# Window attention and MLP, second block: attention output kept by token, 32-row column tiles, input split moved to GpSimd

## What is computed

```
xn  = layernorm(x) ; windows of 8 x 8 tokens (49 to an image, 1568 in all)
qkv = xn @ w_qkv + b_qkv ; 6 heads of 16 features ; q = q / sqrt(16)
p   = softmax(q k^T)                # over the window's 64 keys, per head
x1  = x + (p v) @ w_proj + b_proj
out = x1 + gelu(layernorm(x1) @ w_fc1 + b_fc1) @ w_fc2 + b_fc2     # 384 hidden
```

## Time and profile before

| | us |
|---|---|
| median of 3 runs of the kernel before | 7315.32 |
| lowest and highest of the 3 | 7312.77, 7322.0 |
| span of the profiled execution (its own time; what lies around the span is not recorded) | 7322.4 |
| busy in the span: PE, PE weight loads | 7021.7, 5453.8 |
| busy in the span: DVE, ACT, POOL | 6310.8, 6294.8, 5480.1 |
| first matmul of the second block's set-up | 4462.4 |

### The profile page before, as it was taken

The page is one execution under the profiler, slowest core; times in us unless marked ns, Lnnn a source line. Parts: engine busy times, 40 slices in busy tenths (PEclk is TensorE's granted clock), DMA queues, the critical chain, the costliest instruction groups (busy, mean ns, idle before and its releaser), DMA issues. The chain is left out here.

```text
span 7322.4 us, 312543 instructions
## 1 busy us (share of the span) xinstructions
PE 7021.7 (96%) x110894; PEld 5453.8 (74%) x110894; DVE 6310.8 (86%) x13114; ACT 6294.8 (86%) x11444; POOL 5480.1 (75%) x6349
## 2 busy tenths in 40 slices
PE   6999999999999999999999995999999999999998
PEld 4777777777777777777777774777777777777777
DVE  5888888888888888888888885888888888888886
ACT  5999999999998999999999995877887877877877
POOL 3777777777777777777777775777777777777776
PEclk9999999999999999999999997999999999999999
DMA  0111111111111111111111111111111111111111
GB/s 21 29 30 30 30 29 30 29 29 30 30 30 29 30 30 29 30 30 30 29 30 30 30 26 27 44 44 44 44 44 44 44 44 43 44 44 44 45 44 36
DMA packets 367610, 252.62 MB, mean 34 GB/s; under 512 B 271816, under 2 KB 347336, under 8 KB 366152
## 3 DMA queue, kind: packets, MB, share of 16 engines
q1 hardware_dynamic: 366154, 233.04, 12.4%
HBM read 78.64 MB, written 77.07 MB: 21 GB/s over the span
## 5 line engine op out<-in xcount | busy, mean ns | idle before, releaser
L879 POOL TENSOR_TENSOR swin_score<-swin_score,swin_top 113x588 f32<-113x588 f32 x1024 | 1203.1, 1175 | 744.2 <-DVE swin_top L751 743.5
L622 ACT ACTIVATE swin_probT<-swin_ps_probs 128x339 f32<-128x339 f32 x2048 | 922.0, 450 | 198.7 <-PE swin_ps_probs L479 177.4
L479 PE MATMUL swin_ps_probs<-swin_ident,swin_prob 113*128 113x113 f32 x6144 | 991.8, 270 | 6.7 <-ACT swin_probT L622 6.7
L1564 POOL TENSOR_TENSOR plain_prob<-plain_prob,plain_inv_total 128x384 f32<-128x384 f32 x784 | 634.4, 830 | 450.1 <-DVE plain_inv_total L1477 450.1
L479 PEld LDWEIGHTS swin_ps_probs<-swin_ident,swin_prob 113*128 113x128 f32 x6144 | 667.9, 141 | 355.1 <-issue 320.7
L746 DVE TENSOR_TENSOR swin_score<-swin_ps_scores,swin_bias_tab 113x588 f32<-113x588 f32 x1024 | 777.9, 760 | 175.1 <-PE swin_ps_scores L469 173.8
L751 DVE TENSOR_REDUCE swin_top<-swin_score 113x12 f32<-113x588 f32 x1024 | 769.0, 751 | 0.2
L628 ACT ACTIVATE swin_prob<-swin_score 113x588 f32<-113x588 f32 x1024 | 719.0, 702 | 5.8 <-POOL swin_score L879 2.9
L782 DVE SCALAR_TENSOR_TENSOR swin_x<-swin_y,swin_y_rstd,swin_x_res 98x96 f32<-98x96 f32 x1024 | 601.7, 645 | 0.8 <-POOL swin_y_rstd L897 0.7
L1289 PE MATMUL plain_ps_dense<-plain_w_fc,plain_hid 128*128 128x96 f32 x4704 | 589.1, 275 | 2.2 <-ACT plain_hid L1362 2.2
L493 PEld LDWEIGHTS swin_ps_mixed<-swin_probT,swin_v_heads 128*32 128x32 f32 x24576 | 422.3, 109 | 222.2 <-issue 145.7
(11 more groups left out here) (188 smaller groups left out, 20880.6 us busy)
## 6 DMA issues: line engine op xcount, KB each, us to landing
swin_k_heads<-swin_k_hat SPq DMA_DIRECT2D x1024, 36.8 KB
plain_x_in<-between_blocks SPq DMA_DIRECT2D x784, 48.0 KB, 2.2
plain_k_heads<-plain_k_hat SPq DMA_DIRECT2D x392, 96.0 KB, 2.1
out_dram<-plain_x SPq DMA_DIRECT2D x784, 48.0 KB
swin_x_in<-in_x SPq DMA_DIRECT2D x224, 136.5 KB
between_blocks<-swin_x SPq DMA_DIRECT2D x224, 136.5 KB
swin_x_in<-in_x SPq DMA_DIRECT2D x224, 19.5 KB
between_blocks<-swin_x SPq DMA_DIRECT2D x224, 19.5 KB
```

Of the source, the lines that this page charges most:

```text
L479: last = nc.tensor.transpose(psP[:, n * QT:(n + 1) * QT], prob[0:QT, p, 2 * hp:2 * hp + 2, :].rearrange('p h k -> p (h k)'), ident[0:QT, 0 ...
L622: nc.scalar.activation(to, psP[:, 0:3 * QT], ACT.Copy).then_inc(did['probT'], 1)
L879: nc.gpsimd.tensor_tensor(view, view, bcast(top[0:QT, p % 2, :], 2, WIN), ALU.subtract).then_inc(did['shifted'], 1)
L1564: nc.gpsimd.tensor_tensor(pair, pair, bcast(inv_total[0:QT, p // 2, p % 2 * heads:(p % 2 + 1) * heads], 2, WIN), ALU.mult).then_inc(did['p ...
```

## The change

In the second block, on every group:

- **Mix by token.** The stationary factor is now 32 queries of `probT`, the moving one the 34 columns (`V`) of `v_heads` for a pair of heads: 16 features of each and two columns of ones, which give the sum of the exponentials of each head. The result is token-major in four column tiles of 32 rows, 48 matmuls to a group. DVE takes the reciprocal of the sums from PSUM and multiplies (`scale_mixed`), PE turns the result with four transposes (`turn_mixed`), and DVE copies it to `mixedT` (`copy_mixed`). `total` on DVE, `scale_probs` on POOL and `copy_mixed` on ACT are gone, and `turn_probs` waits for the exponentials themselves.
- **32-row column tiles.** Values, projection and MLP output are issued as matmuls with 32 stationary columns, into rows 0, 32, 64 and 96, instead of 64 or 128 stationary columns. The moving side stays (48, 96 and 96 columns).
- **Input's parts on POOL.** `high_x` goes from ACT and `low_x` from DVE to POOL, where the high part is the input times a column of ones, both from `xT` in SBUF.
- **Orders.** `turn_x1` now stands behind `queries` on PE (ahead of values and mix), values ahead of mix, and `turn_x` behind the MLP output. ACT, DVE and POOL are reordered to suit.

The core of the diff (waits of `turn_x` and `turn_x1` included):

```diff
@@ buffers and set-up
-    HB = J // 2
-    SUMS = 2 * HALF * 2
+    V = 2 * D + 2
...
+one = sb('one', [DIM, 1])
...
-v_heads = sb('v_heads', [128, 2, WINDOWS, BANDS, HB, 32])
+v_heads = sb('v_heads', [128, 2, WINDOWS, HP, V])
...
-total_of = sb('total', [128, 2, 2 * heads])
-inv_total = sb('inv_total', [128, 2, 2 * heads])
+inv_total = sb('inv_total', [128, PAIRS * HP, 2])
+mixed = sb('mixed', [128, PAIRS, DIM])
...
-    part = v_heads[odd * HALF:odd * HALF + WIN, buffer, 0, 0, 0, odd * D:(odd + 1) * D]
-    return bass.AP(part.tensor, part.offset, [list(part.ap[0]), [HB * 32, WINDOWS * BANDS], [32 + 2 * D, HB], [1, D]])
+    part = v_heads[odd * HALF:odd * HALF + WIN, buffer, :, :, odd * D:(odd + 1) * D]
+    return part.rearrange('r w n d -> r (w n) d')
...
+    nc.gpsimd.memset(one[:], 1.0)
...
+            ones = v_heads[odd * HALF:(odd + 1) * HALF, buffer, :, :, 2 * D + odd]
+            nc.vector.memset(ones.rearrange('r w n -> r (w n)'), 1.0)
@@ tensor engine
-            pe.wait_ge(did['mixedT'], upto(g + d - 1))
-            for w in range(WINDOWS):
-                p, half = divmod(w, 2)
-                for band in range(BANDS):
-                    last = nc.tensor.matmul(psO[32 * band:32 * band + 32, w * WIN:(w + 1) * WIN], v_heads[:, parity(d), w, band, 0, :], probT[:, p, band, half * HALF:half * HALF + WIN], start=True, stop=True)
+            pe.wait_ge(did['mixed'], upto(g + d - 1))
+            for p in range(PAIRS):
+                for hp in range(HP):
+                    for rows in range(0, TT, 32):
+                        last = nc.tensor.matmul(psO[rows:rows + 32, (p * HP + hp) * V:(p * HP + hp + 1) * V], probT[:, p, hp, rows:rows + 32], v_heads[:, parity(d), 2 * p + rows // HALF, hp, :], start=True, stop=True)
             last.then_inc(did['mixed_made'], 1)
 
+    def turn_mixed(d):
+        if exists(g + d, groups):
+            pe.wait_ge(did['mixed'], upto(g + d))
+            pe.wait_ge(did['xT_whole'], upto(g + 1))
+            for p in range(PAIRS):
+                last = nc.tensor.transpose(psT[0:DIM, p * TT:(p + 1) * TT], mixed[:, p, :], ident[0:TT, 0:TT])
+            last.then_inc(did['mixed_turned'], 1)
+
     def turn_probs(d, p):
         if exists(g + d, groups):
-            pe.wait_ge(did['prob_scaled'], upto(g + d, p, PAIRS))
+            pe.wait_ge(did['prob'], upto(g + d, p, PAIRS))
...
-            pe.wait_ge(did['xT'], upto(g + d))
+            pe.wait_ge(did['xT_whole'], upto(g + d))
             for w in range(WINDOWS):
                 for odd in range(2):
                     cols = w_qkv[:, 2 * DIM:3 * DIM].rearrange('c (h o d) -> c h o d', o=2, d=D)[:, :, odd, :]
-                    out = psM[odd * HALF:odd * HALF + WIN, bank, w * HP * D:(w + 1) * HP * D]
-                    last = nc.tensor.matmul(out, xT[:, parity(d), w * WIN:(w + 1) * WIN], cols, start=True, stop=True)
+                    for part in range(2):
+                        rows = odd * HALF + 32 * part
+                        first = w * WIN + 32 * part
+                        last = nc.tensor.matmul(psM[rows:rows + 32, bank, w * HP * D:(w + 1) * HP * D], xT[:, parity(d), first:first + 32], cols, start=True, stop=True)
...
-                last = nc.tensor.matmul(psM[0:TT, bank, p * DIM:(p + 1) * DIM], mixedT[0:DIM, parity(d), p * TT:(p + 1) * TT], w_proj[0:DIM, :], start=True, stop=True)
+                for rows in range(0, TT, 32):
+                    last = nc.tensor.matmul(psM[rows:rows + 32, bank, p * DIM:(p + 1) * DIM], mixedT[0:DIM, parity(d), p * TT + rows:p * TT + rows + 32], w_proj[0:DIM, :], start=True, stop=True)
...
-    def output(d, h, bank):
+    def output(d, bank):
         if exists(g + d, groups):
             pe.wait_ge(did['hid'], upto(g + d, CHUNKS - 1, CHUNKS))
-            for p in (2 * h, 2 * h + 1):
+            for p in range(PAIRS):
                 for c in range(CHUNKS):
-                    last = nc.tensor.matmul(psM[0:TT, bank, p * DIM:(p + 1) * DIM], hid[:, c, p * TT:(p + 1) * TT], w_fc2[:, c, :], start=c == 0, stop=c == CHUNKS - 1)
-            if h == 1:
-                last.then_inc(did['fc2_made'], 1)
+                    for rows in range(0, TT, 32):
+                        last = nc.tensor.matmul(psM[rows:rows + 32, bank, p * DIM:(p + 1) * DIM], hid[:, c, p * TT + rows:p * TT + rows + 32], w_fc2[:, c, :], start=c == 0, stop=c == CHUNKS - 1)
+            last.then_inc(did['fc2_made'], 1)
...
-            pe.wait_ge(did['x1T_low'], upto(g - 4))
-            pe.wait_ge(did['xT'], upto(g + d - 1))
+            pe.wait_ge(did['x1T_low'], upto(g - 3))
...
-            pe.wait_ge(did['xT'], upto(g + 2))
-            pe.wait_ge(did['x1T_low'], upto(g + d - 1))
+            pe.wait_ge(did['mixedT'], upto(g - 2))
...
     scores(0)
     turn_probs(-1, 2)
+    turn_mixed(-2)
     free(('hid', -4, 1, CHUNKS), ('x2', -5), ('v_heads', 0), ('k_hat', 0))
     keys(1, A)
     turn_probs(-1, 3)
     free(('hid', -4, 2, CHUNKS), ('x1', -3), ('q_hat', 0))
     queries(1, B)
-    mix(-1)
+    turn_x1(-3)
     free(('k_hat', 1), ('hid', -4, 1, CHUNKS), ('x2', -5), ('v_heads', 0))
     values(1, A)
-    turn_x(2)
+    mix(-1)
     free(('q_hat', 1), ('hid', -4, 2, CHUNKS), ('x1', -3))
     project(-2, B)
     free(('v_heads', 1), ('k_hat', 1), ('hid', -4, 1, CHUNKS), ('x2', -5))
-    output(-4, 0, A)
-    turn_x1(-3)
-    output(-4, 1, A)
+    output(-4, A)
+    turn_x(2)
     free(('x1', -2), ('q_hat', 1), ('hid', -4, 2, CHUNKS))
     hidden(-3, 0, B)
@@ scalar engine
-    def copy_mixed(d):
...
-            nc.scalar.activation(xT[0:DIM, parity(d), 0:NT], psT[0:DIM, 0:NT], ACT.Copy)
-    def high_x(d):
-        if exists(g + d, groups):
-            act.wait_ge(did['q_made'], upto(g + d - 2))
-            nc.scalar.activation(xT_high[:, parity(d), :], psT[0:DIM, 0:NT], ACT.Copy).then_inc(did['xT'], 1)
+            nc.scalar.activation(xT[0:DIM, parity(d), 0:NT], psT[0:DIM, 0:NT], ACT.Copy).then_inc(did['xT_whole'], 1)
...
     copy_turned(-1, 2)
     exponentials(0, 0)
     copy_turned(-1, 3)
     exponentials(0, 1)
-    copy_mixed(-1)
+    high_x1(-3)
     spread_values(1, A)
-    copy_x(2)
-    high_x(2)
     exponentials(0, 2)
     exponentials(0, 3)
-    high_x1(-3)
     act.preload_act_table_set(GELU_SET)
+    copy_x(2)
     gelu(-3, 0, B)
     copy_turned(0, 0)
@@ vector engine
-    def total(d, h):
...
+    def scale_mixed(d):
+        if exists(g + d, groups):
+            dve.wait_ge(did['mixed_made'], upto(g + d))
+            dve.wait_ge(did['mixed_turned'], upto(g + d - 1))
+            made = psO[:, 0:PAIRS * HP * V].rearrange('p (n c) -> p n c', c=V)
+            nc.vector.reciprocal(inv_total[:, :, :], made[:, :, 2 * D:V]).then_inc(did['inv_total'], 1)
+            dve.wait_ge(did['inv_total'], upto(g + d))
+            out = mixed[:, :, :].rearrange('p w (n o d) -> p (w n) o d', o=2, d=D)
+            nc.vector.tensor_tensor(out, made[:, :, 0:2 * D].rearrange('p n (o d) -> p n o d', d=D), bcast(inv_total[:, :, :], 3, D), ALU.mult).then_inc(did['mixed'], 1)
...
-    def low_x(d):
-        if exists(g + d, groups):
-            dve.wait_ge(did['xT'], upto(g + d))
-            dve.wait_ge(did['q_made'], upto(g + d - 2))
-            nc.vector.tensor_tensor(xT_low[:, parity(d), :], xT[0:DIM, parity(d), 0:NT], xT_high[:, parity(d), :].bitcast(F32), ALU.subtract).then_inc(did['xT_low'], 1)
+    def copy_mixed(d):
+        if exists(g + d, groups):
+            dve.wait_ge(did['mixed_turned'], upto(g + d))
+            dve.wait_ge(did['proj_made'], upto(g + d - 2))
+            nc.vector.tensor_copy(mixedT[0:DIM, parity(d), :], psT[0:DIM, 0:NT]).then_inc(did['mixedT'], 1)
...
     shift(0, 0)
+    copy_mixed(-2)
     shift(0, 1)
     bias_k(1, A)
     bias_q(1, B)
     shift(0, 2)
     shift(0, 3)
+    low_x1(-3)
     residual(-2, B)
-    total(0, 0)
-    low_x1(-3)
     partial_x1(-2)
     result(-4, A)
-    total(0, 1)
     moments_x1(-2)
     partial_x(3)
-    low_x(2)
+    scale_mixed(-1)
     moments_x(3)
@@ GpSimd
-    def scale_probs(d, p):
...
+    def high_x(d):
+        if exists(g + d, groups):
+            pool.wait_ge(did['xT_whole'], upto(g + d))
+            pool.wait_ge(did['q_made'], upto(g + d - 2))
+            nc.gpsimd.tensor_tensor(xT_high[:, parity(d), :], xT[0:DIM, parity(d), 0:NT], bcast(one[:, :], 1, NT)[:, :, 0], ALU.mult).then_inc(did['xT'], 1)
+
+    def low_x(d):
+        if exists(g + d, groups):
+            pool.wait_ge(did['xT'], upto(g + d))
+            nc.gpsimd.tensor_tensor(xT_low[:, parity(d), :], xT[0:DIM, parity(d), 0:NT], xT_high[:, parity(d), :].bitcast(F32), ALU.subtract).then_inc(did['xT_low'], 1)
...
+    power_x1(-3)
+    norm_x1(-3)
     power_x(2)
     norm_x(2)
     residual_x(1)
-    power_x1(-3)
-    norm_x1(-3)
-    scale_probs(0, 0)
-    scale_probs(0, 1)
     residual_x1(-3)
-    scale_probs(0, 2)
-    scale_probs(0, 3)
+    high_x(2)
+    low_x(2)
```

19 lines of the change are left out of this document (5 added, 14 removed).

## The result

The changed kernel takes 7578.59 us (median of four runs, 7573.03 to 7588.81) against 7316.58 for the kernel before: 1.0358 of its time, 95% interval 1.0344 to 1.0373. It is slower by 262 us where 211 us less were forecast, and it lies outside the range (7010 to 7270).

What follows compares the result with a forecast made beforehand. PE's own work was taken as the bound; cheaper blocks, less four added transposes and a new stall before values, made 13.00 us a group instead of 14.09, or 211 us over about 194 periods: 7104 us, range 7010 to 7270.

Steps and rivals of the forecast that it cites:

- What bounds the kernel now: Kernel before: PE's own work is the bound, 14.09 us a group without a jump; clock at 2.4 GHz outside block changes.
- the cost of a record: PE's fp32 matmuls: about 0.85 ns per column of the larger side, the other side's load hidden, plus 3 ns per record.
- Where the waits go: PE's idle times of 0.46 and 0.18 us give way to one stall of about 0.54 us before values; `turn_mixed` costs nothing.
- The stall behind `k_hat`: PE before values: about 0.54 us waiting for DVE to free dense bank A, as `copy_mixed` (0.62 us) delays `k_hat`.
- the ring's slack: POOL's chain from `turn_x` to `turn_x1`: ready at 16.1, wanted at 17.2, 1.1 us to spare; each part may take 1.7 us.
- The sum for a group: PE's steps from values to the next scores add up to 13.00 us a group, 1.09 less than 14.09; 211 us in all.
- the pace of pairs: Load-and-multiply pairs on PE: new mix wants 9 ns a pair, values 12, where the trace's fastest sustained pace was 15.4.
- six come in under 40 ns: Burst of six pairs on PE behind a jump with nothing queued for 3.47 us, cited against a 15.4 ns pace limit.
- Rival 2: PE's pairs come no faster than 21.3 ns: a period of 14.8 us, 7453 us in all; chance 0.13.
- The Trainium skill's rule: About 60 cycles overhead per matmul: 288 pairs take 7.2 us instead of 4.33, the program 7660 us; not used as floor.
- rivals 1 and 3: 1: pairs no faster than 15.4 ns, 7267 us, chance 0.15; 3: stall at values small or gone, 7000 to 7045, 0.1.
- the front end: PE's steps from scores up to values, forecast to be set by scores, then DVE, so that values start at 5.18 us.

Runs made afterwards that it cites:

- Run 8: Changed kernel in the spread order, with 64-row projection and output tiles, 64-column values, four value buffers and POOL's residual sum earlier; 7120.08 us, 0.9725 of the kernel before.
- Run 5: Changed kernel with the values (`v_heads`) in four buffers instead of two; 7561.17 us, 1.0329 of the kernel before.
- run 13: Changed kernel with only POOL's residual sum moved to right behind x1's normalising; 7558.59 us, 1.0326 of the kernel before.
- run 11: Run 8 with POOL's residual sum put back behind the input's normalising; 7259.56 us, 0.9918 of the kernel before.
- y_order32: Changed kernel with POOL's residual sum earlier and four value buffers, all tiles still of 32 rows; 7541.84 us, 1.0312 of the kernel before.
- x_order: Run 8 with the changed kernel's order of steps on PE, ACT and DVE; 7223.4 us, 0.9868 of the kernel before.
- the spread order: Changed kernel with values before keys, mix between keys and queries, and four value buffers; 7367.43 us, and 7374.53 with ACT's copy of the last probabilities earlier.

## Why the prediction was wrong, point by point

**What bounds the kernel now: right**, and so was the cost of a record. 0.85 ns for each column of the larger side, with the load of a 32-column tile hidden, gives mix in 0.88 us (0.84 forecast), values in 0.71 (0.79), output in 2.11 (2.01). The forecast had added some 0.08 us to mix and values for the start of a block and nothing to the output, and its projection is 8 x 84 = 0.67, not 0.69; these are slips of up to 0.1 us. Run 8 repeats the output with half the records. What did not hold is that the clock stays at the 2.4 GHz level outside the change of blocks. The trace of the kernel before already shows a fall: behind the 3.47 us of idle time of the earlier trace rows the granted clock is 0.50 (6657.50 to 6660.70 us), and the scores take 1.88 us (6657.24 to 6659.12) instead of 1.05.

**Where the waits go: nearly right.** The stall behind `k_hat` came, 0.31 us instead of 0.54; `copy_mixed` on DVE takes 0.68 us (0.62 forecast), and the `turn_mixed` step costs nothing on its own. What I did not see: values now stand ahead of mix, so the buffer that ACT spreads them into is read by the mix right behind them; ACT waits for that mix, the output waits for ACT to free the values' bank, and that is 0.31 us a group. It was not in the sum. Run 5 gives it 17 us. POOL's two parts, and the copy, are these (busy us, mean ns, idle before):

```profile
L1576 POOL TENSOR_TENSOR plain_xT_high<-plain_xT,plain_one 96x512 fp32r<-96x512 f32 x173 | 179.4, 1037 | 928.9 <-ACT plain_xT L1400 928.9
...
L1581 POOL TENSOR_TENSOR plain_xT_low<-plain_xT,plain_xT_high 96x512 fp32r<-96x512 f32 x173 | 221.7, 1281 | 13.6
...
L1521 DVE COPY plain_mixedT<-plain_ps_turn 96x512 f32<-96x512 f32 x173 | 117.2, 677 | 2.7 <-PE plain_ps_turn L1253 2.7
```

1.04 and 1.28 us for the 1.2 each that I took. I called the ring's slack 1.1 us for `turn_x1`. I left out its other half, the residual sum on POOL that SP's load and the spreading of keys stand behind; it cost 20 us in the changed kernel (run 13) and 140 in a faster order (run 11).

**The sum for a group: the step that failed.** It priced each block by the array and had no term for how fast instructions arrive. I had the question before me, as the pace of pairs, and answered it with the earlier trace rows and with "six come in under 40 ns". Six pairs are twelve instructions behind a pause of 3.47 us; such a burst says how fast PE takes what already lies there, and nothing of a run of 576. At the higher clock the pace held as forecast while instructions were there: 96 pairs in 0.88 us. What failed is that the blocks stand back to back. The missing term is 1.38 us a group of "issue", and it is more than the 1.09 that I had as gain. In the pair that differs in tiles alone (y_order32 against x_order) it is 1.64 us with what follows from it. The second missing term hangs on the first: some 0.4 us a group at the lower clock behind the idle stretches. With the 0.31 us of the values' bank these are 2.1 of the 2.5 us by which a mean group (15.6 us with the jumps) is longer than forecast (13.0, and 0.1 for the jumps); the rest is not assigned.

**Rival 2 (slower) had the sign** and its time, 7453, is half the way: +138 of the +262 us. Its mechanism is not the one that the runs show. It has each pair slow, 21.3 ns; in the trace pairs are at 9.2 ns and then nothing comes for up to 2.5 us. In run 8 the mix's 96 pairs take 0.99 us (6001.41 to 6002.40), where this rival has 2.04, and nothing is idle behind them. I gave it 0.13 because the earlier trace rows have 15.4 ns, a row that could not speak against idle stretches in a long run of instructions. The Trainium skill's rule (TensorEngine Tiling, Instruction Overhead), about 60 cycles for a matmul, points the right way for this change, but as a floor of 25 ns a pair it does not hold here: 96 pairs took 0.88 us in four column tiles. By it, as an estimate, the mix of run 8 would take 2.4 us instead of 0.99, and its group 14.4 us instead of 13.03.

**What was open between rivals 1 and 3** has no bearing on it: neither pace nor the front end set the time.

What is left open: how far ahead PE's instruction blocks are asked for, and so from how many instructions in how many us on a stretch comes. In the changed kernel's last 2.55 ms no two blocks land closer than 3.16 us, 12.3 ns for each of 256 instructions, where the dense run wants one each 7.6 ns. In other kernels single pairs of blocks land 1.3 to 2.4 us apart, so this is not shown to be a limit. Open is also why the median stretch in the spread order is of 0.9 to 1.0 us where it is 1.1 to 1.7 in the order of the change with 750 instructions. No run varied the place of a block's edge within the loop.

## What to carry to other kernels

Beside the array's time of each block write its number of instructions, loads included, and look at the longest run of short ones: with 576 in 4.4 us (7.6 ns each) this kernel lost 1.4 us a group, with 384 in some 5 us (x_order, 13 ns each) 0.1. No row of the kernel before could show that, but a doubled instruction count should have made me price it. Price an idle time of PE of over 1 us also by the clock that it can cost behind it. Take the widest stationary tile at which the moving side still binds (64 rows against 96 moving columns: same time, half the instructions), and put long products between dense blocks. And when a step moves on the engine that releases the next load, follow that load to its last reader, not only to the next step on PE.
